# Turning four layers' weights one product earlier, and a batch of graph convolutions over 100 columns instead of 128 in its first group

## The reference, cut to what matters

```python
# block 1: five layers of message passing with a GRU cell, on each of the 16 graphs
A = (adj != 0)
for l in range(5):
    m   = h @ weight[l]
    agg = einsum('bij,bid->bjd', A, m)
    gi, gh = agg @ w_ih.T + b_ih, h @ w_hh.T + b_hh
    r, z = sigmoid(i_r + h_r), sigmoid(i_z + h_z)
    n = tanh(i_n + r * h_n)
    h = (1 - z) * n + z * h
x = layernorm(x + h * mask)

# block 2: five groups of the first 25 nodes, sizes 25, 9, 7, 6, 6; two graph convolutions each
for g, idx in enumerate(GROUPS):
    norm_adj = sym_normalised(adj[idx, idx] + I)
    t     = relu(norm_adj @ (x[idx] @ W1[g]) + b1[g])      # 128 -> 256
    out_g = relu(norm_adj @ (t @ W2[g]) + b2[g])           # 256 -> 128
    fused[idx] += softmax(fusion_w)[g] * out_g
out = layernorm(x + fused)
```

## Time and profile before

| | us |
|---|---|
| median of 3 runs (lowest, highest) | 495.66 (495.07, 495.97) |
| the profiled execution, whole | 494.41 |
| its span in the profile | 492.7 |

### The profile page before, as it was taken

The page is one execution under the profiler, slowest core; times in us unless marked ns, Lnnn a source line. Parts: engine busy times, 40 slices in busy tenths (PEclk is TensorE's granted clock), DMA queues, the critical chain, the costliest instruction groups (busy, mean ns, idle before and its releaser), DMA issues.

```text
span 492.7 us, 7178 instructions
## 1 busy us (share of the span) xinstructions
PE 481.3 (98%) x2301; PEld 229.1 (47%) x2301; DVE 353.2 (72%) x659; ACT 303.6 (62%) x537; POOL 334.0 (68%) x378
## 2 busy tenths in 40 slices
PE   7999999999999999999999999999999999999994
PEld 5344444444444444444444444444444444564554
DVE  3767867696866687778687768877668675445796
ACT  4556655655655566777667776476755767645564
POOL 3654774748775698997689658659996766224466
PEclk9999999999999999999999999999999999999998
DMA  8868252565535547264955477323453233322313
GB/s 277 259 164 157 45 150 56 152 162 129 123 64 154 109 95 185 56 136 105 191 107 151 111 205 172 66 44 82 89 111 79 48 65 63 65 43 44 80 45 86
DMA packets 133676, 55.72 MB, mean 113 GB/s; under 512 B 97297, under 2 KB 125414, under 8 KB 133638
## 3 DMA queue, kind: packets, MB, share of 16 engines
q1 hardware_dynamic: 108356, 32.39, 32.2%
q10 hardware_dynamic: 25282, 22.87, 15.3%
HBM read 27.46 MB, written 4.19 MB: 64 GB/s over the span
## 4 chain that ended last, share of the span: by engine, by line
PE 81%; POOL 6%; DVE 4%; DMA 4%; ACT 3%; issue 2%; SPq 0%; POOLq 0%; DVEq 0%; ACTq 0%
PE pA L788 24%; PE pR L793 6%; PE pR L794 6%; PE pR L795 6%; PE pZ L795 6%; PE pZ L793 6%; PE pZ L794 6%; PE pHN L793 3%; PE pIN L793 3%; PE pHN L795 3%; PE pHN L794 3%; PE pIN L794 3%; PE pIN L795 3%; POOL ZH L527 2%; POOL HT L538 1%
## 5 line engine op out<-in xcount | busy, mean ns | idle before, releaser
L538 POOL TENSOR_TENSOR HT<-H,HT 128x512 f16<-128x512 f32 x76 | 91.2, 1200 | 91.8 <-ACT HT L1160 91.7
L788 PE MATMUL pA<-A,NAT 128*128 128x512 fp8e4 x640 | 151.0, 379 | 0.0
L527 POOL TENSOR_TENSOR ZH<-Z,H 128x512 f32<-128x512 f32 (+1 forms) x80 | 102.9, 1286 | 28.7 <-ACT Z L1175 27.1
L1414 DVE SCALAR_TENSOR_TENSOR T<-pHN,BHN,R 128x512 f32<-128x512 f32 (+1 forms) x80 | 59.9, 749 | 78.1 <-ACT R L1167 77.8
L1180 ACT ACTIVATE pIN<-T,COLS 128x512 f32<-128x512 f32 (+1 forms) x80 | 55.3, 691 | 72.1 <-DVE T L1418 72.0
L788 PEld LDWEIGHTS pA<-A,NAT 128*128 128x128 f16 x640 | 62.5, 98 | 74.9 <-issue 1.0
L1160 ACT ACTIVATE HT<-H 128x512 f16<-128x512 f32 x76 | 47.8, 629 | 64.7 <-DVE H L1428 64.6
L1424 DVE SCALAR_TENSOR_TENSOR pIN<-Z,pIN 128x512 f32<-128x512 f32 (+1 forms) x80 | 55.1, 688 | 24.4 <-ACT pIN L1180 24.3
L1167 ACT ACTIVATE R<-pR,BRZ 128x512 f32<-128x512 f32 (+1 forms) x80 | 54.3, 679 | 19.9 <-PE pR L795 19.3
L1428 DVE TENSOR_TENSOR H<-ZH,pIN 128x512 f32<-128x512 f32 (+1 forms) x80 | 54.8, 685 | 10.2 <-POOL ZH L527 7.9
L1408 DVE TENSOR_TENSOR AG<-pA,AG 128x512 f16<-128x512 f32 x80 | 54.8, 684 | 8.2 <-ACT AG L1156 8.2
(11 more groups left out here) (284 smaller groups left out, 811.8 us busy)
## 6 DMA issues: line engine op xcount, KB each, us to landing
AS<-in_adj_dram ACTq DMA_DIRECT2D x13, 1024.0 KB, 5.9
XR<-in_x_dram ACTq DMA_DIRECT2D x16, 256.0 KB, 3.0
XS<-in_x_dram ACTq DMA_DIRECT2D x13, 256.0 KB, 3.5
out_dram<-Y SPq DMA_DIRECT2D x16, 192.0 KB, 2.3
AS<-in_adj_dram SPq DMA_DIRECT2D x2, 1024.0 KB, 8.3
AS<-in_adj_dram SPq DMA_DIRECT2D x4, 256.0 KB, 5.4
NAT<-HT SPq DMA_TRANSPOSE x64, 3.2
XS<-in_x_dram SPq DMA_DIRECT2D x3, 256.0 KB, 7.4
```

Source lines behind the costliest of these rows:

```text
L527: g_.tensor_tensor(ZH[:, cs], Z[:, cs], H[:, b, cs], ALU.mult).then_inc(zh_p, 1)
L538: g_.tensor_tensor(HT[:, b, 1, :], H[:, b, :], HT[:, b, 0, :], ALU.subtract).then_inc(h_lo, 1)
L788: last = mm(pA2[:, k % 2, :], NAT[:, k % 2, h, i, :], A8[:, b, i, :], start=(h == 0 and i == 0), stop=(h == 1 and i == NI - 1))
L1414: v.scalar_tensor_tensor(out=T[:, cs], in0=pHN[:, cs], scalar=BHN[:, 0:1], in1=R[:, cs], op0=ALU.add, op1=ALU.mult).then_inc(t_v, 1)
```

## The change

Two edits, independent of one another.

1. The four transposes of the weights (`turn_weights`) leave `between(2)` and are called in step 2 ahead of `gates_of_state(2)`, with their two waits.
2. Group 0 of the batch takes `FULL = Q * 25 = 100` columns instead of 128, so `WIDE` becomes 212. The copies on GpSimd, the matmuls of "A01", "A2", "B0", "B1", "S" and ScalarE's reads follow. "T", "D" and "sum" keep their sizes, and `STB` its slots of 32.

```diff
-WIDE = P + PACK
+FULL = Q * len(GROUPS[0])
+WIDE = FULL + PACK
...
@@ GpSimd, prepare_batch
-                    g_.tensor_copy(BDA[:, :, 0:P].rearrange("p c (q n) -> p c q n", q=Q), BD[:, 0, 0:TAIL, :, :])
+                    g_.tensor_copy(BDA[:, :, 0:FULL].rearrange("p c (q n) -> p c q n", q=Q),
+                                   BD[:, 0, 0:TAIL, :, 0:len(GROUPS[0])])
...
@@ TensorE, batch
+            full = pC[:, 0:TAIL * FULL].rearrange("p (c x) -> p c x", c=TAIL)
...
-                    mm(wide[0], W1S[:, 0, h * P:(h + 1) * P], YTB[:, :, 0:P], start=True, stop=True).then_inc(g_mm, 1)
+                    mm(full, W1S[:, 0, h * P:(h + 1) * P], YTB[:, :, 0:FULL], start=True, stop=True).then_inc(g_mm, 1)
...
-                        last = mm(wide[0], W2S[:, 0, h, :], H1B[:, h, :, 0:P], start=(h == 0), stop=(h == NH - 1))
+                        last = mm(full, W2S[:, 0, h, :], H1B[:, h, :, 0:FULL], start=(h == 0), stop=(h == NH - 1))
...
@@ TensorE, between and the loop
             def between(k):
-                if k == 2:
-                    pe.wait_ge(ld_wl, 16)
-                    pe.wait_ge(cols_v, 1)
-                    for l in range(1, L):
-                        last = tr(pC[:, (l - 1) * D:l * D], WL[:, l, :], IDF[:, :])
-                    last.then_inc(wl_t, 1)
...
+            def turn_weights():
+                pe.wait_ge(ld_wl, 16)
+                pe.wait_ge(cols_v, 1)
+                for l in range(1, L):
+                    last = tr(pC[:, (l - 1) * D:l * D], WL[:, l, :], IDF[:, :])
+                last.then_inc(wl_t, 1)
...
                 if 2 < k < K - 1:
                     aggregate(k + 1)
+                if k == 2:
+
+                    turn_weights()
                 gates_of_state(k)
                 between(k)
...
@@ ScalarE, batch
-                    fn(H1B[:, h, :, 0:P], wide[0], ACT.Relu, bias=B1[:, 0, h:h + 1]).then_inc(g_ea, 1)
+                    fn(H1B[:, h, :, 0:FULL], full, ACT.Relu, bias=B1[:, 0, h:h + 1]).then_inc(g_ea, 1)
...
                     fn(STB[:, :, 0:P].rearrange("p c (q n) -> p c q n", q=Q)[:, :, :, 0:n],
-                       wide[0].rearrange("p c (q n) -> p c q n", q=Q)[:, :, :, 0:n], ACT.Copy).then_inc(g_ea, 1)
+                       full.rearrange("p c (q n) -> p c q n", q=Q), ACT.Copy).then_inc(g_ea, 1)
```

More of the change, by code:

```diff
@@ L596, in prepare_batch @@
                         j = 0
-                        dst = BDA[:, :, P + SLOT[g - 1]:P + SLOT[g]].rearrange("p c (q j) -> p c q j", q=Q)
+                        dst = BDA[:, :, FULL + SLOT[g - 1]:FULL + SLOT[g]].rearrange("p c (q j) -> p c q j", q=Q)
                         for run in runs_of(GROUPS[g]):
@@ L947, in batch @@
                     tr(pC[:, P:P + G], ROWS[0:G, :], IDF[0:G, 0:G]).then_inc(g_mm, 1)
-                    mm(short, SEL, BDA[:, :, P:WIDE], start=True, stop=True).then_inc(g_mm, 1)
+                    mm(short, SEL, BDA[:, :, FULL:WIDE], start=True, stop=True).then_inc(g_mm, 1)
                 elif stage == "A01":
@@ L968, in batch @@
                     for g in range(1, G):
-                        last = mm(packed(short, g), W1S[:, g, h * P:(h + 1) * P], packed(YTB[:, :, P:WIDE], g),
+                        last = mm(packed(short, g), W1S[:, g, h * P:(h + 1) * P], packed(YTB[:, :, FULL:WIDE], g),
                                   start=True, stop=True)
@@ L980, in batch @@
                         for h in range(NH):
-                            last = mm(packed(short, g), W2S[:, g, h, :], packed(H1B[:, h, :, P:WIDE], g),
+                            last = mm(packed(short, g), W2S[:, g, h, :], packed(H1B[:, h, :, FULL:WIDE], g),
                                       start=(h == 0), stop=(h == NH - 1))
@@ L1251, in batch @@
                     act.wait_ge(g_dv, 1)
-                    fn(H1B[:, h, :, 0:P], wide[0], ACT.Relu, bias=B1[:, 0, h:h + 1]).then_inc(g_ea, 1)
+                    fn(H1B[:, h, :, 0:FULL], full, ACT.Relu, bias=B1[:, 0, h:h + 1]).then_inc(g_ea, 1)
                     act.wait_ge(g_mm, BATCH_MM[stage + "b"])
                     for g in range(1, G):
-                        last = fn(packed(H1B[:, h, :, P:WIDE], g), packed(short, g), ACT.Relu, bias=B1[:, g, h:h + 1])
+                        last = fn(packed(H1B[:, h, :, FULL:WIDE], g), packed(short, g), ACT.Relu, bias=B1[:, g, h:h + 1])
                     last.then_inc(g_ea, 1)
@@ L1262, in batch @@
                     fn(STB[:, :, 0:P].rearrange("p c (q n) -> p c q n", q=Q)[:, :, :, 0:n],
-                       wide[0].rearrange("p c (q n) -> p c q n", q=Q)[:, :, :, 0:n], ACT.Copy).then_inc(g_ea, 1)
+                       full.rearrange("p c (q n) -> p c q n", q=Q), ACT.Copy).then_inc(g_ea, 1)
                     act.wait_ge(g_mm, BATCH_MM["Sb"])
-                    fn(STB[:, :, P:WIDE], short, ACT.Copy).then_inc(g_ea, 1)
+                    fn(STB[:, :, P:P + PACK], short, ACT.Copy).then_inc(g_ea, 1)
                 elif stage == "T":
@@ L1600, in batch_matrices @@
                 v.tensor_scalar(STB[:, :, BIAS_ROW], pC[:, P:P + 1].to_broadcast([P, TAIL]), FW[:, 0:1], None, ALU.mult)
-                link(v.tensor_tensor(STB[:, :, WIDE:WIDE + G - 1],
+                link(v.tensor_tensor(STB[:, :, P + PACK:P + PACK + G - 1],
                                      pC[:, None, P + 1:P + G].to_broadcast([P, TAIL, G - 1]),
```

## The result

| | before | after |
|---|---|---|
| median of 17 runs each (lowest to highest) | 494.30 (493.90 to 498.53) | 493.09 (492.77 to 495.26) |
| ratio after / before, 95% interval | | 0.9969 (0.9956 to 0.9982) |
| the profiled execution (span) | 494.41 (492.7) | 493.06 (491.3) |

The change gains 1.2 us by the medians and 1.5 us by the ratio (0.9 to 2.2 us). The forecast gain of 1.14 us holds. The three runs of the kernel before that stood ahead of the prediction (495.66 in the middle) were high ones of the 17.

What follows compares the result with a forecast made beforehand. TensorE, busy 98% of the span, was taken as the bound; 0.43 us for the transposes plus 0.71 for the columns gave 1.14 us, so 494.5 us from the 495.66 median (493.27 from the profiled execution), range 493.8 to 495.5.

Steps and rivals of the forecast that it cites:

- the last one of the sum: Whole kernel: the 1.14 us gain taken from the 495.66 median of the runs shown, giving 494.52 us.
- What bounds the kernel: Whole span: TensorE, busy 98%, so work taken off it or put into its gaps counts in full.
- Edit 1: Step 2: four weight transposes fit into the 1.13 us gap behind HT<-NAT, worth 0.43 us, bounds 0 to 0.60.
- Edit 2: Batch, group 0: 420 f32 columns fewer on TensorE at 1.68 ns each, worth 0.71 us.
- a weight load of 0.190 us was no floor: 212-column passes: if loads could not overlap, 0.08 us instead of 0.14; the prediction put the floor at or below 0.105.
- The low end of 0.50 for this edit: Batch: gain from the columns if the eight 300-column passes run a tenth slower than the line.
- Rival A: Step 2: usual gap too short to hide the transposes, only the columns count, 494.95 us; chance 0.17.
- Rival B: Whole kernel: TensorE isn't the bound, removed work only uncovers a wait, 495.6 us; chance 0.11.
- the rule that it held against itself: Whole kernel: judged by weight-load share, 47%, TensorE has room, VectorE at 72% is most contended, neither edit shows.
- Rival C: Step 2: weights land late and TensorE waits, one for one after 22.40; slower, 497.6 us; chance 0.06.

Runs made afterwards that it cites:

- e4: The kernel before, word for word, timed against itself: 494.16 us beside 494.21, ratio 1.0001.
- e5: The kernel before with the weights of layers 1 to 4 loaded later, behind HT<-NAT of graph 2: 494.31 us beside 494.14, ratio 1.0001.
- e11: The changed kernel again, both edits, on the chip of the held-load runs: 493.09 us against 494.28 for the kernel before, ratio 0.9977.
- e2: The kernel before with only group 0's columns cut, transposes in the old place: 493.54 us against 494.21, ratio 0.9986.
- e9: The changed kernel with the 1 MB load of graph 3's adjacency held back on ScalarE: 492.43 us against 494.28 for the kernel before, ratio 0.9962.
- e1: The kernel before with only the four weight transposes moved: 494.00 us against 494.21, ratio 0.9999.
- e7: The changed kernel with the four weight transposes done four times over in their new place: 493.64 us against 494.14 for the kernel before, ratio 0.9991.
- e6: The changed kernel with the weights loaded later, behind HT<-NAT of graph 2: 496.03 us against 494.14 for the kernel before, ratio 1.0031.
- e8: The changed kernel with NAT's low half of graph 2 ahead of ZH on GpSimd: 493.02 us against 494.14 for the kernel before, ratio 0.9982.
- e3: The changed kernel as it is, both edits: 493.20 us against 494.21 for the kernel before, ratio 0.9980.
- e12: The kernel before, neither edit, with the 1 MB load of graph 3's adjacency held back: 493.36 us against 494.37, ratio 0.9976.

## Why the prediction was right or wrong

**The step that failed** is the last one of the sum: "The median of the runs shown, 495.66, lies 1.25 above the profiled one; the same gain from it gives 494.52." The gain was right and was taken off the wrong level. Three runs were taken for the level of the kernel, and the range around them allowed 0.3 us for it. Seventeen runs have the middle at 494.30, e4 and the other sessions 494.14 to 494.37. The profiled execution, 494.41, was the better witness, and the text had it: 494.41 - 1.14 = 493.27 us and a span of 491.56 were worked out there, against 493.09 and 491.3 measured. That the profiled execution was "the fastest of those shown" I read as a reason to trust the others; four values from 494.41 to 495.97, where all the gain is 1.14, should have made the range reach to the lowest of them less the gain, 493.3 and under. By its own terms the range would have begun at 494.35 - 0.3 = 494.05; the 493.8 has no working, and it wasn't enough either.

Why single executions are longer stays open for the most part. Two profiles caught moderately long ones: that of e5 (495.05, the highest of its ten runs, median 494.31) and that of e11 (493.55, median 493.09). In both, VectorE's cast of graph 1's adjacency waited for its load, 0.31 and 0.74 us, and step 1's `pR` on the aggregate came 5.95 and 6.38 us after step 0's, against 5.61 in all other traces. The cast in e4, then in e11:

```profile
13.50 1.28 DVE L1402 TENSOR_SCALAR A<-AS 128x1024 fp8e4<-128x1024 f32 x2
```

```profile
14.14 1.29 DVE L1410 TENSOR_SCALAR A<-AS 128x1024 fp8e4<-128x1024 f32 x2 [0.74 <-DMA AS<-in_adj_dram]
```

No profile caught an execution that was a whole microsecond above its median.

**What bounds the kernel**: right. Everything taken off TensorE's list or put into its gap came back in full at the next step mark and stayed up to the end (e2: 0.70 us at step 76; e9: 0.64 at step 2). One sentence under it said too much, "Everywhere else its next matmul starts when the one before has streamed": from start to start the trace of before has eight hold-ups of 0.09 to 0.54 us beside the gap in its 80 steps, 1.7 us together, and the earlier trace rows show 0.6 of them. They cost the forecast nothing.

**Edit 1**: place, cover and size right. The transposes ran from the end of the aggregate for 0.43 us, both semaphores were there, and the copy on VectorE and the merge had their slack. Forecast 0.43, in the traces 0.54 with the scatter of the landing, in the timing not resolved (e1). The merge of step 3 starts at 32.41, 0.14 us earlier than before in an execution that began 0.35 us later.

**Edit 2**: right. 0.71 forecast, 0.70 in every pair of traces, 0.67 timed. The line through 240 and 384 columns held at 300 (0.50 us) and 212 (0.36 us), and a weight load of 0.190 us was no floor for passes of 0.178. The low end of 0.50 for this edit was not needed.

**Rival A** (no room in the usual execution) fell with e7. **Rival B** fell with e2 and e9: 0.64 to 0.70 us taken from TensorE's timeline were 0.66 and 0.67 us of the whole, though weight loads fill only 47% of it. The prediction took half of the rule that it held against itself: the Trainium skill ("Perfetto Trace Analysis", Identifying the Most-Contended Engine) asks for MFU, the matmul work done as a share of the peak, beside the share of weight loads. My estimate of how full TensorE's timeline is, from the trace: 26 matmuls of 512 columns in each of 80 steps, at a pitch of 0.216 us, are 449 us, 91% of the span. Read so, TensorE is near its limit, as the runs found; the weight-load share alone misled. **Rival C**: the mechanism is as described and was made to happen by e6; in the kernel as it is the load lands 3.3 us early.

**What the prediction didn't see** is that the gap itself was the larger prize: it took 5.64 us for what the DMA does in 3.2, and the earlier trace rows showed that number beside nothing to measure it by. The list of issues on the page of the profile has 3.2 us for the 64 transposes `NAT<-HT`, and the 13 later `HT<-NAT` of that trace took 3.0 to 4.0 us.

## What to carry to other kernels

A move into a gap is worth what fits, and only as long as the gap is there: ask first what makes the gap, since removing it can be worth more (here 1.0 us by one wait, where the move gained 0.4 to 0.5), and the two gains don't add. A forecast of a gain well under 1% needs its level from many executions or from the profiled one, and a range that covers the spread of the level before that of the gain. Here it paid to hold back for 2 us a load that nobody needed for 8.9 us, issued just ahead of a smaller transfer that the busiest engine waited for; it was left with 0.2 us to spare.

## What the runs showed of the hardware that I had not expected

A DMA transpose of 256 KB issued 0.1 to 0.9 us behind a 1 MB load took 5.5 to 6.3 us and landed 0.8 to 1.1 us behind it (e8: issued 0.6 us earlier, 0.7 us longer); issued 1.1 us or more ahead of the load it took 3.1 to 3.2 us, and the load 6.3 to 6.7 instead of 5.5 to 5.9. So the order of issue between the two queues decided who finished first. And six small hold-ups of TensorE of 0.1 to 0.55 us (ahead of `pIN` in steps 15, 34, 36, 45 and 63, ahead of `pHN` in step 39) come back in every trace of every version, while others of 0.1 to 0.25 us (steps 53 and 55 before, 18 in e3, 41 in e12) come in one execution only; a difference of 0.3 us between two profiles needs a third one before it is put down to an edit.
